# Decoder layer: quantised products with the weights' scaling on GpSimd, row norms and the first round's last outputs on ScalarE, and 16-bit halves of the rounded words turned in place

## The chip, the cores and the metric

The kernel runs on one core of a Trainium2 chip. The metric is the time of one execution on the device, in microseconds (us), as the median of several runs. The engines named below are TensorE (PE in the rows), VectorE (DVE), ScalarE (ACT), GpSimd (POOL) and SyncE (SP), which issues the DMAs. Each has its own instruction stream; semaphores order them.

## What is computed

The input x has four batches of 512 rows and 512 columns. Three blocks are added to it, each on a layer norm of what came before: an attention with low-rank projections and rotary parts, then a quantised expert per batch, then a top-2 mixture of eight experts. The change touches the second:

```
def smooth_quant_linear(x, w):
    s  = sqrt(max(amax_x_by_column, 1e-6) / max(amax_w_by_column, 1e-6)); s = max(s, 1e-6)
    xs, ws  = x / s, w * s
    x_scale = max(row max |xs|, 1e-6) / 127      # w_scale in the same way, from ws
    x_q = clip(round(xs / x_scale), -127, 127)   # w_q in the same way
    return x_q @ w_q.T * x_scale * w_scale.T

h = smooth_quant_linear(layernorm(x), fside[b])      # 512 columns in, 512 out
gate, up = split(h)
y = smooth_quant_linear(silu(gate) * up, ctx[b])     # 256 columns in, 512 out
x = x + y
```

## The kernel before, in words

Attention runs first and ends with projections of output rows, which VectorE adds to x (`add_y`). Its last projections and the beginning of the quantised stage are interleaved by hand in the functions called `tail`. After the quantised stage the mixture of experts runs over 16 row tiles of 128 rows.

The quantised stage works on two batches at a time: round r = 0, 1, linear layer l = 0, 1 (512 or 256 input columns, `LIN`), batch u = 0, 1 of the round. The list `HALVES` orders them as (r, l, u) = (0,0,0), (0,0,1), (0,1,0), (0,1,1), (1,0,0) and so on: eight halves. PSUM banks 4u to 4u+3 belong to batch u. Each engine has a loop over `HALVES`, written out in order; in it, `preceding(h)` is the half before and `succeeding` of that one is the next layer of the other batch, whose channel maxima are found meanwhile. The time at which one half's input products begin on VectorE is taken as its start below, and the halves are numbered 1 to 8.

What happens to one half:

- `channels` (TensorE, L822) turns the rows of inputs and of weights by transposes in 32-bit words; `scales` (VectorE, L663) takes the maxima by column (L675), joins them (L679), and computes the factor with a root on GpSimd (`root`, L452). `spread` (L839, matmul at L845) puts 1/s and s on all partitions, into two banks.
- `quantise` (VectorE, L695): kind 0 multiplies the input rows by 1/s in place (L709, four tiles), takes the maximum of each row (L711), and makes the scale and its reciprocal (L712, L713). Kind 1 does the same for the weights and writes the products to `HF[u]`.
- ScalarE's `rounded` (L525, L534) multiplies by the reciprocal and adds 12582912, which rounds to a whole number in a 32-bit word; `whole` (L536, L544) subtracts it and writes bf16 into a buffer (`QX[u]` for inputs, the space of the raw weights for weights).
- `quantised_t` (TensorE, L849, L857) turns these bf16 rows with `identb`, and `transposed` (ScalarE, L547, L554) copies them from PSUM to `QXT` and `QWT`. `row_scale` (L861) spreads the weights' row scales, `output_scales` (L558) copies them to `WSB`.
- `layer` (TensorE, L869, L876) multiplies. `outputs` (VectorE, L715, L721), called in the next half, scales by row and column in one operation out of PSUM into `HF[u]`.
- After layer 0, `silu` (ScalarE, L562) and `gate_product` (GpSimd, L463, L466) make the input of layer 1. After layer 1, `residual` (GpSimd, L470, L474) adds `HF[u]` to x; the last one is on VectorE (L727).
- The norm of a round's rows: `norm_stats` (L631) and `norm_batch` (L642) on VectorE, a root on GpSimd (L460), `norm_rows` (L654, L659) on VectorE, four tiles. For round 1 it stands in the middle of `scales`.

VectorE's order in a half is: input products, weight products, outputs of the half before, norm batch if the next layer is a first one, scales of the next. ScalarE's is: round inputs, copy them, round weights, silu, copy out the turned inputs, copy the weights, output scales, copy out the turned weights; at the end of halves 3 and 4 a cast of expert weights of 4096 columns (L520).

Of the kernel before, what the change touches and what calls it, by code (L numbers as in the profile page):

```python
# [17 lines left out]
B, L, D = 4, 512, 512  # L18
# [13 lines left out]
ROUND = 12582912.0  # L32
# [3 lines left out]
def decoder_layer(nc, x, fside, ctxw, w_qa, q_norm_w, w_qb, w_kva, kv_norm_w, w_kvb, w_o,  # L36
# [16 lines left out]
    with es:  # L53
# [243 lines left out]
        QX = [take(TB * D, bf16) for _ in range(2)]  # L297
# [25 lines left out]
        qeps, qrs = sm[1][:, 70:74], sm[1][:, 74:78]  # L323
# [22 lines left out]
        qx_r, qw_r, v_bc, l_mm, l_out = (sem(n) for n in ("qx_r", "qw_r", "v_bc", "l_mm", "l_out"))  # L346
# [36 lines left out]
        def rounded_rows(l, u, kind):  # L383
            return QX[u] if kind == 0 else (WF[u] if l == 0 else WC[u]).bitcast(bf16)[:, 0:TB * D]
# [65 lines left out]
        def later_pool(pool):  # L450
# [25 lines left out]
            for u in range(2):  # L476
                first_root(0, u)
            for r, l, u in HALVES:
                if l == 0:
                    gate_product(r, u)  # L480
                    root(r, 1, u)
                else:
                    if r + 1 < B // 2:
                        first_root(r + 1, u)
                    if r + 1 < B // 2 or u == 0:
                        residual(r, u)
# [28 lines left out]
        def later_act(act):  # L515
# [6 lines left out]
            def rows_of(l, u, kind):  # L522
                return (NX[u] if l == 0 else AG[u]) if kind == 0 else HF[u]

            def rounded(r, l, u, kind):  # L525
# [4 lines left out]
                rows, iv = rows_of(l, u, kind), IV[u][kind]  # L530
                act.wait_ge(own, li * 4 + 4)
# [3 lines left out]

            def whole(r, l, u, kind):  # L536

                wid, li = LIN[l][0], layer_of(r, l, u)
                made, done = ((x_q, qx_r), (w_q, qw_r))[kind]
                stride = wid if kind == 0 else D  # L540
                rows = rows_of(l, u, kind)
                for t in range(TB):
                    act.wait_ge(made, li * TB + t + 1)
                    act.activation(rounded_rows(l, u, kind)[:, t * D:t * D + wid], rows[:, t * stride:t * stride + wid],  # L544
                                   ACT.Copy, bias=-ROUND).then_inc(done, 1)

            def transposed(r, l, u, kind):  # L547
# [4 lines left out]
                for k in range(2):  # L552
                    act.wait_ge(tr, li * TB + 2 * k + 2)
                    act.activation(dst[u].rearrange("p (c t q) -> p t c q", c=DC, t=TB)[:, 2 * k:2 * k + 2, 0:c],  # L554
                                   bankb[4 * u + k].rearrange("p (t c q) -> p t c q", t=2, c=DC)[:, :, 0:c],
                                   ACT.Copy).then_inc(te, 1)
# [62 lines left out]
        def later_dve(dve, tail):  # L619
# [22 lines left out]
            def norm_batch(r, u):  # L642

                s = r * 2 + u
                dve.wait_ge(q_stat, 2 * s + 2)
                dve.memset(qcar, 0.0)
# [3 lines left out]
                dve.wait_ge(q_agg, s + 1)  # L650
                dve.tensor_scalar(qeps, qmv.rearrange("p (t a) -> p t a", a=2)[:, :, 1], 1e-5, None, ALU.add)\
                    .then_inc(q_var, 1)

            def norm_rows(r, u):  # L654

                s = r * 2 + u
                dve.wait_ge(q_rstd, s + 1)
                for t in range(TB):
                    dve.tensor_scalar(NX[u][:, t * D:(t + 1) * D], xall(batch_of(r, u) * TB + t),  # L659
                                      qmv[:, 2 * t:2 * t + 1], qrs[:, t:t + 1], ALU.subtract, ALU.mult)\  # L660
                        .then_inc(q_norm, 1)

            def scales(r, l, u, beside=None):  # L663
# [6 lines left out]
                for t in range(2 * TB):  # L670
                    if t == TB and l == 0 and r > 0:
                        norm_rows(r, u)
# [22 lines left out]
            def quantise(r, l, u, kind):  # L695
# [3 lines left out]
                vlink = chain(own_, li, 4)  # L699
                src = (NX[u] if l == 0 else AG[u]) if kind == 0 else (WF[u] if l == 0 else WC[u])  # L700
                dst, sc = ((src, XM[u]), (HF[u], WM[u]))[kind]
                m3 = src.rearrange("p (t n) -> p t n", t=TB)
                d3 = dst.rearrange("p (t n) -> p t n", t=TB)
                iv = IV[u][kind]
                dve.wait_ge(v_bc, li * 2 + 1 + kind)
                if l == 0 and kind == 1 and r > 0:
                    dve.wait_ge(x2_made, r * 2 - 1 + u)
                for t in range(TB):
# [1376 lines left out]
```

## Time and profile before

| | us |
|---|---|
| median of three runs | 1169.33 (1169.28 to 1170.31) |
| profiled execution, span from the first to the last instruction | 1169.4 |
| busy: TensorE matmuls | 980.4 (84%) |
| busy: VectorE | 959.2 (82%) |
| busy: ScalarE | 678.1 (58%) |
| busy: GpSimd | 296.4 (25%) |

The profiled execution has no separate time on record; its span stands for it. Busy is the sum of the instructions' durations on an engine. These shares are means over attention (to about 890 us), the quantised stage (to 1046.8 us) and the mixture (to the end), which have different limits.

### The profile page before, as it was taken

The numbers are of one execution on the slowest core, as the hardware profiler recorded it, in microseconds if no ns is written. First come the engines' busy times: TensorE is split into PE (matmuls) and PEld (weight loads), VectorE is DVE, ScalarE is ACT, GpSimd is POOL, SyncE is SP. The second block draws the span as 40 slices with busy tenths as digits, with TensorE's granted clock in tenths as the row PEclk, the third lists the DMA queues.
The fourth block names the chain that finished last, engine by engine and source line by source line (L and its number), as shares of the span: only waits on it lengthen the run. The fifth ranks groups of instructions, "written<-read, shape, count | busy, mean of one in ns | idle before, by whom it ended". The sixth has DMA issues, their size and how long they took to land.

```text
span 1169.4 us, 18715 instructions
## 1 busy us (share of the span) xinstructions
PE 980.4 (84%) x6106; PEld 574.0 (49%) x6124; DVE 959.2 (82%) x2669; ACT 678.1 (58%) x1449; POOL 296.4 (25%) x524
## 2 busy tenths in 40 slices
PE   0446667899999999999999999999978655559997
PEld 0234444555555555555555555555545544435553
DVE  5757749989989888989998988888868898866885
ACT  1446557667667666756666666656512676754442
POOL 1036533223223223222322222213100113221211
PEclk9769779999999999999999999999989888769999
DMA  9300003433323336334335244336363520001333
GB/s 350 139 1 1 1 8 73 75 59 71 71 59 67 66 62 142 62 64 69 65 68 138 55 68 60 64 67 140 68 218 86 168 91 19 0 1 36 84 80 91
DMA packets 217328, 90.78 MB, mean 78 GB/s; under 512 B 191496, under 2 KB 202760, under 8 KB 216720
## 3 DMA queue, kind: packets, MB, share of 16 engines
q1 hardware_dynamic: 217232, 89.58, 33.5%
q8 instruction: 50, 0.82, 0.3%
q14 instruction: 46, 0.38, 0.1%
HBM read 36.06 MB, written 7.34 MB: 37 GB/s over the span
## 4 chain that ended last, share of the span: by engine, by line
PE 53%; DVE 30%; ACT 6%; issue 5%; POOL 3%; DMA 3%; SPq 0%; DVEq 0%; ACTq 0%; POOLq 0%
PE bank L1930 13%; PE bank L1880 8%; PE bank L1915 6%; PE bank L1828 3%; PE bank L1859 3%; DVE arena L709 2%; PE bank L1898 2%; DVE arena L711 2%; PE bank L1901 2%; PE bank L1899 2%; PE bank L1900 2%; PE bank L1902 2%; DVE arena L791 2%; DVE arena L675 2%; DVE arena L1529 2%
## 5 line engine op out<-in xcount | busy, mean ns | idle before, releaser
L1218 ACT ACTIVATE arena<-bank,arena,scal 128x128 f32<-128x128 f32 (+3 forms) x256 | 157.7, 616 | 112.7 <-POOL arena L1059 111.6
L1930 PE MATMUL bank<-arena 128*128 128x512 f16 x768 | 179.1, 381 | 1.9 <-DVE arena L1562 1.9
L1536 DVE SCALAR_TENSOR_TENSOR arena<-arena 128x128 f16<-128x128 f32 (+3 forms) x256 | 142.2, 555 | 9.1
L1059 POOL TENSOR_TENSOR arena<-arena,scal 128x1 f32<-128x1 f32 x256 | 51.7, 203 | 347.4 <-DVE arena L1512 345.7
L1880 PE MATMUL bank<-arena 128*128 128x512 f16 x576 | 137.6, 385 | 0.0
L1529 DVE TENSOR_SCALAR arena<-arena 128x128 f16<-128x128 f32 (+3 forms) x256 | 125.4, 490 | 7.4 <-DVE arena L1521 0.8
L1512 DVE TENSOR_REDUCE arena<-bank 128x1 f32<-128x128 f32 (+3 forms) x256 | 123.7, 483 | 7.8 <-PE bank L1903 6.7
L1915 PE MATMUL bank<-arena 128*128 128x512 f16 (+3 forms) x768 | 117.7, 304 | 11.5 <-DMA arena<-arena 5.8
L1930 PEld LDWEIGHTS bank<-arena 128*128 128x128 f16 x768 | 72.9, 98 | 81.0 <-issue 4.4
L1915 PEld LDWEIGHTS bank<-arena 128*128 128x128 f16 x768 | 71.8, 99 | 63.0 <-issue 16.5
L1237 ACT ACTIVATE arena<-bank 32x512 f32<-32x512 f32 x128 | 75.3, 588 | 26.0 <-PE bank L1859 24.7
L1898 PE MATMUL bank<-arena 128*128 128x128 f16 (+3 forms) x256 | 77.0, 301 | 9.1 <-DVE arena L1429 5.0
L1880 PEld LDWEIGHTS bank<-arena 128*128 128x128 f16 x576 | 54.4, 99 | 55.8 <-issue 3.5
L1249 ACT ACTIVATE arena<-arena 64x512 f16<-64x512 f32 x128 | 79.9, 624 | 1.2
L1902 PE MATMUL bank<-arena 128*128 128x128 f16 (+3 forms) x256 | 76.9, 300 | 0.0
L1900 PE MATMUL bank<-arena 128*128 128x128 f16 (+3 forms) x256 | 76.9, 300 | 0.0
L1901 PE MATMUL bank<-arena 128*128 128x128 f16 (+3 forms) x256 | 76.9, 300 | 0.0
L1899 PE MATMUL bank<-arena 128*128 128x128 f16 (+3 forms) x256 | 76.9, 300 | 0.0
L1228 ACT ACTIVATE arena<-bank 128x512 f16<-128x512 f32 x64 | 38.2, 596 | 65.8 <-PE bank L1880 65.5
L835 PE MATMUL bank<-identf,arena 128*128 128x128 f32 x192 | 37.7, 355 | 40.8 <-DVE arena L721 35.9
L1828 PE MATMUL bank<-arena 128*128 128x384 f16 (+1 forms) x384 | 54.8, 303 | 18.1 <-DVE arena L1386 15.7
L1064 POOL TENSOR_TENSOR arena<-arena 128x512 f32<-128x512 f32 x32 | 44.9, 1404 | 94.2 <-ACT arena L1237 94.1
(201 smaller groups left out, 2049.5 us busy)
## 6 DMA issues: line engine op xcount, KB each, us to landing
arena<-in_L_attn_w_qb SPq DMA_DIRECT2D x1, 4608.0 KB, 21.6
arena<-arena SPq DMA_TRANSPOSE x272, 2.7
arena<-in_x SPq DMA_DIRECT2D x4, 1024.0 KB, 6.9
arena<-in_L_attn_w_o SPq DMA_DIRECT2D x1, 4096.0 KB, 31.9
arena<-in_fside_BxS2xS SPq DMA_DIRECT2D x4, 1024.0 KB, 8.8
arena<-in_L_ffn_w SPq DMA_DIRECT2D x8, 512.0 KB, 7.6
out<-arena SPq DMA_DIRECT2D x16, 256.0 KB, 2.3
arena<-in_x SPq DMA_DIRECT2D x12, 256.0 KB, 3.0
```

The source lines that it names most:

```text
L1218: act.activation(pf(k), banks[S_BANKS[G % 3]][:, 0:n], ACT.Exp, bias=NB[:, k:k + 1], scale=sc_exp, accum_out=SUM[:, k:k + 1]).then_inc(s_e ...
L1512: dve.tensor_reduce(NEGM[:, (g & 3):(g & 3) + 1], banks[S_BANKS[G % 3]][:, 0:n], AX.X, ALU.max, negate=True).then_inc(s_max, 1)
L1529: dve.tensor_scalar(ph_part(k, 0), pf(k).rearrange("p (t c) -> p t c", c=P), R4[:, k:k + 1], None, ALU.mult).then_inc(s_hi, 1)
L1536: dve.scalar_tensor_tensor(out=ph_part(k, 1), in0=pf(k).rearrange("p (t c) -> p t c", c=P), scalar=R4[:, k:k + 1], in1=ph_part(k, 0), op0= ...
L1880: last = pe.matmul(banks[Q_BANK][:, :], wq(a, c, (i & 7) * 2 + h), ct(bp, b, c, 0, L), start=(k == 0), stop=(k == 3 * QC - 1))
L1898: pe.matmul(bank[:, 0:n], qn(h, 0, q, P), ct(bp, 0, QC, 0, n), start=True, stop=False)
L1899: pe.matmul(bank[:, 0:n], qn(h, 0, q, P), ct(bp, 1, QC, 0, n), start=False, stop=False)
L1900: pe.matmul(bank[:, 0:n], qn(h, 1, q, P), ct(bp, 0, QC, 0, n), start=False, stop=False)
L1901: pe.matmul(bank[:, 0:n], qr(j, h, q, P), kr(bp, 0, 0, n), start=False, stop=False)
L1902: pe.matmul(bank[:, 0:n], qr(j, 2, q, P), kr(bp, 1 + h, 0, n), start=False, stop=False)
L1915: last = pe.matmul(banks[O_BANK][:, kt * P:L], cn(bp, a, kt), pt(h, b, kt, kt * P, L - kt * P), start=(kt == 0 and n == 0), stop=(kt == TB ...
L1930: last = pe.matmul(banks[Y_BANK][:, :], ot(gp, a, k, (q & 3) * P, P), wo(b, gp * GH + k), start=(k == 0 and n == 0), stop=(k == GH - 1 and ...
```

## The change

The weight products of `quantise` move to GpSimd (`weight_products`), which cannot read them from the PSUM bank, so ScalarE first copies the factors into a buffer `SSB` (`weight_factors`). The norm rows move to ScalarE (`norm_rows`), as x * rstd + (-mean * rstd), with the second term from GpSimd (`norm_factors`). The outputs of layer 1 of round 0 are made by ScalarE (scaled by row, `scaled_outputs`) and then GpSimd (scaled by column, `output_rows`). The constant added in rounding becomes 12582912 + 26112, so that the low 16 bits of the 32-bit word, read as fp16, are 1536 plus the whole number. TensorE turns these halves where they lie, every second 16-bit word (`rounded_tile`), with `ident16`; ScalarE subtracts 1536 in the copy out of PSUM. `whole` and its eight copies a half, and the buffer `QX`, go. VectorE's order in a half is now: input products, then the outputs of the half before or the norm batch, then the row maxima of the weights, then scales.

```diff
-ROUND = 12582912.0
+SHIFT = 1536.0
+ROUND = 12582912.0 + 26112.0
...
+        def rounded_tile(l, u, kind, t, q):
+            o = t * (LIN[l][0] if kind == 0 else D) + q * P
+            return scaled_rows(l, u, kind).bitcast(fp16).rearrange("p (n h) -> p n h", h=2)[:, o:o + P, 0]
+        def outputs_on_act(r, l):
+            return l == 1 and r + 1 < B // 2
...
             if after is not None:
-                sp.wait_ge(w_t, after * TB + TB)
+                sp.wait_ge(w_prod, after * TB + TB)
...
@@ later_pool @@
+            def norm_factors(r, u):
+                s = r * 2 + u
+                pool.wait_ge(q_var, s + 1)
                 pool.tensor_tensor(qrs, qeps, half, ALU.pow).then_inc(q_rstd, 1)
+                pool.wait_ge(q_rstd, 2 * s + 1)
+                pool.tensor_tensor(qnr, qneg, qrs, ALU.mult).then_inc(q_rstd, 1)
+            def weight_products(r, l, u):
+                wid, li = LIN[l][0], layer_of(r, l, u)
+                src = WF[u] if l == 0 else WC[u]
+                pool.wait_ge(ssb_made, li + 1)
+                if l == 1:
+                    pool.wait_ge(act_m, (r * 2 + u) * TB + TB)
+                elif r > 0:
+                    pool.wait_ge(x2_made, r * 2 - 1 + u)
+                for t in range(TB):
+                    pool.tensor_tensor(HF[u][:, t * D:t * D + wid], src[:, t * wid:(t + 1) * wid],
+                                       SSB[u][:, 0:wid], ALU.mult).then_inc(w_prod, 1)
+            def output_rows(r, u):
+                for t in range(TB):
+                    pool.wait_ge(l_out, layer_of(r, 1, u) * TB + t + 1)
+                    pool.tensor_tensor(HF[u][:, t * D:(t + 1) * D], HF[u][:, t * D:(t + 1) * D], WSB[u],
+                                       ALU.mult).then_inc(o_row, 1)
...
+            norm_factors(0, 0)
+            root(0, 0, 0)
+            norm_factors(0, 1)
+            for h in HALVES:
+                weight_products(*h)
+                prev = preceding(h)
+                after = (0, 0, 1) if prev is None else succeeding(prev)
+                if prev is not None and prev[1] == 0:
+                    gate_product(prev[0], prev[2])
+                if prev is not None and prev[1] == 1 and after is not None:
+                    norm_factors(after[0], after[2])
+                    output_rows(prev[0], prev[2])
+                if after is not None:
+                    root(*after)
+                if prev is not None and prev[1] == 1:
+                    residual(prev[0], prev[2])
...
@@ later_act @@
+            def weight_factors(r, l, u):
+                act.wait_ge(v_bc, li * 2 + 2)
+                act.activation(SSB[u][:, 0:wid], banks[4 * u + 3][:, 0:wid], ACT.Copy).then_inc(ssb_made, 1)
+            def norm_rows(r, u):
+                act.wait_ge(q_rstd, 2 * s + 2)
+                for t in range(TB):
+                    act.activation(NX[u][:, t * D:(t + 1) * D], xall(batch_of(r, u) * TB + t), ACT.Identity,
+                                   bias=qnr[:, t:t + 1], scale=qrs[:, t:t + 1]).then_inc(q_norm, 1)
+            def scaled_outputs(r, l, u):
+                for t in range(TB):
+                    act.wait_ge(l_mm, li * TB + t + 1)
+                    act.activation(HF[u][:, t * D:(t + 1) * D], out_bank(u, t)[:, :], ACT.Copy,
+                                   scale=XM[u][:, t:t + 1]).then_inc(l_out, 1)
...
+            norm_rows(0, 0)
+            norm_rows(0, 1)
             for h in HALVES:
+                weight_factors(r, l, u)
+                if prev is not None and outputs_on_act(*prev[0:2]):
+                    scaled_outputs(*prev)
                 rounded(r, l, u, 0)
-                whole(r, l, u, 0)
-                rounded(r, l, u, 1)
                 if prev is not None and prev[1] == 0:
                     silu(prev[0], prev[2])
+                rounded(r, l, u, 1)
                 transposed(r, l, u, 0)
-                whole(r, l, u, 1)
+                if prev is not None and outputs_on_act(*prev[0:2]):
+                    norm_rows(prev[0] + 1, prev[2])
                 output_scales(r, l, u)
                 transposed(r, l, u, 1)
...
@@ later_dve @@
                 if prev is not None:
                     quantise(r, l, u, 0)
+                    if not outputs_on_act(*prev[0:2]):
+                        outputs(*prev)
+                    elif after is not None:
+                        norm_batch(after[0], after[2])
                 quantise(r, l, u, 1)
-                if prev is None:
-                    scales(0, 0, 1)
-                else:
-                    outputs(*prev)
-                    after = succeeding(prev)
-                    if after is not None:
-                        if after[1] == 0:
-                            norm_batch(after[0], after[2])
-                        scales(*after, beside=(1, after[2]) if after[0:2] == (0, 1) else None)
+                if after is not None:
+                    scales(*after, beside=(1, after[2]) if after[0:2] == (0, 1) else None)
```

In `quantise`, kind 1 no longer multiplies; it waits for `w_prod` and takes the row maxima. In both layers the transposes of rounded rows (`quantised_t`) wait for `x_q` and `w_q`, the rounding itself.

## Rows read from the trace of the kernel before

**Rows 1.** Windows, halves 2 to 7: start:end and length, busy by engine, PEclk.

```profile
910.92:932.37 21.45, 13.00 (x87) 9.65 (x88) 19.24 (x38) 15.13 (x26) 3.48 (x5) 0.76 0.44 121
932.37:948.69 16.32, 11.10 (x64) 8.15 (x66) 14.96 (x39) 11.05 (x26) 3.48 (x5) 0.79 0.17 60
948.69:968.07 19.38, 10.38 (x74) 8.46 (x73) 16.60 (x44) 13.65 (x23) 3.68 (x4) 0.91 0.52 163
968.07:991.85 23.78, 12.16 (x97) 10.21 (x97) 20.99 (x44) 14.26 (x22) 6.69 (x5) 0.86 0.00 1
991.85:1012.75 20.90, 12.90 (x85) 9.87 (x85) 17.07 (x33) 14.27 (x25) 6.46 (x6) 0.76 0.00 0
1012.75:1028.51 15.76, 11.62 (x65) 8.62 (x65) 12.78 (x33) 10.32 (x26) 3.48 (x5) 0.78 0.00 1
```

**Rows 2.** Chain that ended last, halves 1 and 2: start us, us, what.

```profile
889.62 1.78 PE bank L845 x16
...
897.37 2.40 DVE arena L709 x4
...
910.92 2.49 DVE arena L709 x4
...
916.14 2.38 DVE arena L709 x4
...
921.18 2.74 DVE arena L721 x4
```

**Rows 3.** The same chain, half 2's tail to half 7's start.

```profile
928.89 0.25 DVE arena L679 x2
...
932.37 1.32 DVE arena L709 x4
...
935.35 1.31 DVE arena L709 x4
...
943.90 0.42 DVE arena L675
...
957.80 2.38 DVE arena L675 x4
960.19 1.82 DVE arena L659 x4
...
964.44 0.28 DVE arena L679 x2
...
968.07 2.49 DVE arena L709 x4
...
1009.92 0.25 DVE arena L679 x2
```

**Rows 4.** Timeline of ScalarE: start us, us, engine, line, operation, shapes, count.

```profile
947.36 3.63 ACT L520 ACTIVATE arena<-arena 128x4096 bf16<-128x4096 f32 x1
951.71 1.70 ACT L534 ACTIVATE arena<-arena 128x256 f32<-128x256 f32 x4 [0.72 <-DVE arena L713]
973.32 2.56 ACT L534 ACTIVATE arena<-arena 128x512 f32<-128x512 f32 x4 [4.59 <-DVE arena L713]
983.45 1.94 ACT L554 ACTIVATE arena<-bank 128x1024 bf16<-128x1024 bf16 x2 [2.44 <-PE bank L857]
1049.62 0.81 ACT L591 ACTIVATE arena<-arena 128x512 f32<-128x512 f32 x1 [6.17 <-POOL arena L498]
```

**Rows 5.** L1064 on GpSimd, in attention: count, ns min/median/max.

```profile
L1064 POOL TENSOR_TENSOR arena<-arena x32: 1263/1270/1662, 153.4 to 830.7; 128x512 f32<-128x512 f32 x32
```

**Rows 6.** Timeline of GpSimd, gate products and a residual.

```profile
940.45 2.78 POOL L466 TENSOR_TENSOR arena<-arena 128x256 f32<-128x256 f32 x4 [9.94 <-ACT arena L565]
...
966.52 4.54 POOL L474 TENSOR_TENSOR arena<-arena 128x2048 f32<-128x2048 f32 x1
```

**Rows 7.** Lines by form, 890 to 1047 us, transposes: busy us, mean ns.

```profile
L835 PE MATMUL bank<-identf,arena 128*128 128x128 f32 x160 | 33.4, 371 | 40.6 <-DVE arena L721 35.9 <-DVE arena L675 2.1 <-DVE arena L659 1.7
...
L857 PE MATMUL bank<-identb,arena 128*128 128x128 bf16 x192 | 18.6, 251 | 4.5 <-ACT arena L544 3.9
```

More of the change, by code:

```diff
@@ L296, in decoder_layer @@
         place[0] = odd_at
-        QX = [take(TB * D, bf16) for _ in range(2)]
+        SSB = [take(D) for _ in range(2)]
         QXT = [take(DC * L, bf16) for _ in range(2)]
@@ L322, in decoder_layer @@
         pcar = sm[0][:, 84:85]
-        qeps, qrs = sm[1][:, 70:74], sm[1][:, 74:78]
+        qeps, qrs, qneg, qnr = (sm[1][:, 70 + 4 * k:74 + 4 * k] for k in range(4))
         place[0] = moe
@@ L345, in decoder_layer @@
         x_q, x_t, x_te, w_q, w_t, w_te = (sem(n) for n in ("x_q", "x_t", "x_te", "w_q", "w_t", "w_te"))
-        qx_r, qw_r, v_bc, l_mm, l_out = (sem(n) for n in ("qx_r", "qw_r", "v_bc", "l_mm", "l_out"))
+        ssb_made, w_prod, o_row, v_bc, l_mm, l_out = (
+            sem(n) for n in ("ssb_made", "w_prod", "o_row", "v_bc", "l_mm", "l_out"))
         w_row, x_own, w_own = (sem(n) for n in ("w_row", "x_own", "w_own"))
@@ L529, in rounded @@
                 stride = wid if kind == 0 else D
-                rows, iv = rows_of(l, u, kind), IV[u][kind]
-                act.wait_ge(own, li * 4 + 4)
+                rows, iv = scaled_rows(l, u, kind), IV[u][kind]
+                act.wait_ge(own, li * 4 + 4 if kind == 0 else li * 3 + 3)
                 for t in range(TB):
@@ L534, in rounded @@
                     act.activation(w, w, ACT.Copy, bias=ROUND, scale=iv[:, t:t + 1]).then_inc(made, 1)
[L536 to L545, printed above, removed]
             def transposed(r, l, u, kind):
@@ L645, in norm_batch @@
                 dve.wait_ge(q_stat, 2 * s + 2)
+                if s > 0:
+                    dve.wait_ge(q_norm, s * TB)
                 dve.memset(qcar, 0.0)
@@ L650, in norm_batch @@
                 dve.wait_ge(q_agg, s + 1)
+                dve.tensor_scalar(qneg, qmv.rearrange("p (t a) -> p t a", a=2)[:, :, 0], -1.0, None, ALU.mult)
                 dve.tensor_scalar(qeps, qmv.rearrange("p (t a) -> p t a", a=2)[:, :, 1], 1e-5, None, ALU.add)\
                     .then_inc(q_var, 1)
[L654 to L661, printed above, removed]
             def scales(r, l, u, beside=None):
@@ L698, in quantise @@
                 own_ = (x_own, w_own)[kind]
[L699 to L708, printed above, removed]
-                    last = dve.tensor_tensor(d3[:, t, 0:wid], m3[:, t, :], banks[4 * u + 2 + kind][:, 0:wid], ALU.mult)
-                vlink(last)
+                vlink = chain(own_, li, 4 - kind)
+                sc, iv = (XM[u], WM[u])[kind], IV[u][kind]
+                d3 = scaled_rows(l, u, kind).rearrange("p (t n) -> p t n", t=TB)
+                if kind == 0:
+                    dve.wait_ge(v_bc, li * 2 + 1)
+                    if l == 0 and r > 0:
+                        dve.wait_ge(l_out, layer_of(r - 1, 1, u) * TB + TB)
+                    for t in range(TB):
+                        last = dve.tensor_tensor(d3[:, t, 0:wid], d3[:, t, 0:wid], banks[4 * u + 2][:, 0:wid], ALU.mult)
+                    vlink(last)
+                else:
+                    dve.wait_ge(w_prod, li * TB + TB)
                 vlink(dve.tensor_reduce(sc, d3[:, :, 0:wid], AX.X, ALU.max, apply_absolute_value=True))
@@ L727, in outputs @@
                     dve.tensor_tensor(X, X, HF[u], ALU.add).then_inc(x2_made, 1)
-            tail(norm_stats, norm_batch, norm_rows, scales, quantise)
+            tail(norm_stats, norm_batch, scales, quantise)
             for h in HALVES:
@@ L850, in quantised_t @@
                 wid, li = LIN[l][0], layer_of(r, l, u)
-                made, done = ((qx_r, x_t), (qw_r, w_t))[kind]
+                made, done = ((x_q, x_t), (w_q, w_t))[kind]
                 for t in range(TB):
@@ L1755, in _, with tail @@
             out_lo(2 * NPAIR - 1)
-            def tail(norm_stats, norm_batch, norm_rows, scales, quantise):
+            def tail(norm_stats, norm_batch, scales, quantise):
                 add_y(NPAIR - 5)
@@ L1761, in tail @@
                 norm_batch(0, 0)
-                norm_rows(0, 0)
                 add_y(NPAIR - 4)
```

40 lines of the change are left out of this document (13 added, 27 removed).

## Prediction

> **What bounds the kernel now.** Of the span the change touches only the quantised stage, from about 890 us to 1046.8 us. I read it first by stages of one half each [rows 1]. The stage has eight halves; half 1 overlaps the end of attention, halves 2 to 7 take 21.45, 16.32, 19.38, 23.78, 20.90 and 15.76 us, half 8 the rest. In each VectorE is the fullest engine (19.24 of 21.45, 12.78 of 15.76), ScalarE follows (15.13, 10.32), GpSimd is nearly empty (3.5 to 6.7). Busy shares alone don't say what ends a half, so the chain of waits comes next [rows 2, 3]. It runs on VectorE almost without a break: the products and reductions of the input rows, the same for the weight rows, the outputs of the half before (2.74), the channel reductions (0.43 for 256 columns, 2.38 for four of 512), then the short tail of small operations, a root on GpSimd and a spread on TensorE, after which the next half begins. That tail is 3.48 us long in halves 2 and 3 (928.89 to 932.37, norm statistics lie in it), 2.83 in halves 6 and 7 (1009.92 to 1012.75), 3.63 ahead of a half of 512 columns (964.44 to 968.07) [rows 3]. So what leaves VectorE counts fully, until a chain through ScalarE and GpSimd becomes longer.
>
> **What the change removes from VectorE.** The weight products: 2.38 us in each half of 512 columns, 1.31 in each of 256 [rows 2, 3]. The outputs of the first round's second products in halves 4 and 5: 2.74 each [rows 2]. The norm rows in halves 4 and 5: 1.82 each [rows 3]; two more such groups lie under TensorE's last projections and free nothing. Added are one 4-wide negation per norm batch, some 0.1. Sum for halves 1 to 7: 4 x 2.38 (1, 2, 5, 6) + 3 x 1.31 (3, 4, 7) + 2 x 4.56 = 22.6 us.
>
> **What it adds elsewhere.** ScalarE copies the factors out of PSUM, and makes the outputs and norm rows: four tiles of 512 go in 2.56 us as the scaling by a column does now, four of 256 in 1.70; a copy out of the transposes of 512 columns takes 1.94 [rows 4]. It loses eight whole-number copies a half. GpSimd makes four products of a row tile. The same operation takes 1.27 us at the median of 32, once 1.66 [rows 5]; four of 256 go in 2.78 and the residual of 2048 columns in 4.54 [rows 6], so one of 512 goes in 1.24 and four in 4.95 by the line through these two. I take 4.95, nearest to the median; the upper end is 6.6 (4 x 1.66).
>
> I now lay out each half, from the start of its input products (time 0) to that of the next. Input part: 5.22 us (910.92 to 916.14) or 2.98 (932.37 to 935.35). Weight part without the products: 921.18 - 916.14 - 2.38 = 2.66, or, like the input part, 2.98 - 1.32, about 1.6 [rows 2, 3].
>
> *Half 1.* The factors are spread at 891.4 (889.62 + 1.78), copied by 892.0, products done by 897.0; VectorE gets there at 897.37, after the last projection [rows 2]. Nothing is late: it saves 2.4.
>
> *Half 2.* Factors copied by 1.5, products done at 6.5. VectorE: 5.22, outputs to 7.96, weight part to 10.6 (the products are 1.4 early), eight reductions of 0.43 to 14.0, tail 3.48. The gate products wait on GpSimd behind the weight products and behind silu, and are done at about 10; the transposes that need them are 0.5 later, before VectorE asks. 17.5, against 21.45: 3.95 saved, of which 1.7 is VectorE's present wait for those transposes.
>
> *Half 3.* 2.98 + 2.74 + 1.6 + 3.43 + 3.48 = 14.2, against 16.32: 2.1. The outputs come before the weight part now, so they could wait for the layer of half 2; its last tile lands at about 4.3, when the last output begins.
>
> *Half 4.* First place with a new wait. ScalarE ends half 3 with a cast of 3.63 us [rows 4]: scales of the weights known at 7.3, then 1.70 of rounding, 1.0 for the turned inputs, 0.6 for the output scales, 1.4 for the turned weights with TensorE ahead of them, and the cast, 15.6 in all, which is 1.4 of half 4. The factors' copy stands behind the cast, then four products of 256 columns: done at 4.55. VectorE is ready at 3.6 (2.98, and some 0.6 for a norm batch of seven operations like the two small ones of 0.28) [rows 3] and waits 1.0. Weight part to 6.2. Then ScalarE rounds the weights (to 8.0), copies the turned inputs (to 9.0) and only then makes the norm rows (to 11.5). Behind them wait the transposes (0.45) and the last reduction (0.6): 12.6, where VectorE alone would be at 6.2 + 4.8 = 11.0. With the tail of 3.63: 16.3, against 19.38: 3.1 saved. If norm rows run at the 0.81 of the lone operation with a column as bias [rows 4], it is 0.7 less.
>
> *Half 5.* GpSimd's queue is norm factors, output rows, root, residual, and the weight products stand behind the residual, which begins at the root's end (12.6 + 1.95 for small operations and root) and takes 4.7: over at 19.3, which is 3.0 of half 5. Products done at 8.05, where VectorE is ready at 5.9: it waits 2.2. Weight part to 10.7, rounding to 13.3, turned copies to 15.2, norm rows to 17.7, transposes and last reduction to 18.8, tail to 22.5, against 23.78: 1.3 saved.
>
> *Half 6.* Again behind a residual (over at 3.0): products at 8.0; VectorE with the outputs is there at 7.96. 7.96 + 2.7 + 3.43 + 2.83 = 16.95, against 20.90: 3.9.
>
> *Half 7.* 2.98 + 2.74 + 1.6 + 3.43 + 2.83 = 13.6, against 15.76: 2.2.
>
> *Half 8.* The outputs (2.74) now stand ahead of the weight part on the path to the last rounding; the product (1.31) and one set of whole-number copies (at most the 1.70 that four of 256 take) leave it. Even: 0.
>
> Sum: 2.4 + 3.95 + 2.1 + 3.1 + 1.3 + 3.9 + 2.2 = 18.95 us. So 22.6 leave VectorE, some 4.5 of present idle time goes too (VectorE's waits for transposes, which the gate products no longer hold up), and 8.1 come back: waits in halves 4 (1.0 and 1.6) and 5 (2.2 and 3.3 from the weight part to the last norm row). The profiled span is 1169.4 and the median of the runs 1169.33, so they can be taken as one. 1169.4 - 18.95 = 1150.4; for hand-overs between engines that I counted at nothing I add 0.6: **1151**.
>
> **Unknown costs.** The turned halves: TensorE reads every second 16-bit word. No row shows that. Nearest are the 16-bit transposes at 251 ns and those of 4-byte words at 371 [rows 7]. At the second price 16 transposes gain 0.12 x 16 = 1.9 in modelled duration, about 0.9 in pace; most lie beside VectorE, and where they don't (halves 3 and 8, with 4 and 5 possibly) it costs 0 to 2 us in all. I take 0, the price of the row with the same word and shape. A gain is excluded: nothing is read or turned less. GpSimd's products at 1.66 would add 1.7 to each of halves 1, 5 and 6, 0.3 to half 2 and 0.8 to half 4: 6.2. Norm rows at 0.81 for each: 1.4 in halves 4 and 5 together.
>
> The residual of 4.54 us on GpSimd starts at 966.52 [rows 6], and VectorE's products at 968.07, which run inside it, take 2.49, as against 2.38 at 916.14 and 1.31 for half as many columns [rows 2, 3]: no lock is to be seen, only 0.1. The Trainium skill ("SBUF — State Buffer", on the two sides and their ports) says that VectorE in a two-port mode, or with two SBUF inputs, and GpSimd exclude each other for a whole instruction. VectorE's long operations here read at most one operand from SBUF, so by that rule they are free, and the sum stays; its small ones could wait, which is rival C. On strided reads the same page says that 16-byte lines give full speed with two hits or more in a line; every second halfword has four, so the sum stays at the price of contiguous reads. No row here shows either case.
>
> **Rivals.** *A*, the forecast: VectorE's load sets the halves but for 4 and 5. 1149 to 1153.5. *B*: the chain through GpSimd and ScalarE is longer than laid out (products at up to 1.66, norm rows at 0.81, transposes at the wide price): 6.2 + 1.4 + 2 = 9.6 at most, half of it likely, 1153.5 to 1159. For it: half 5 and 6 already end on GpSimd. Against: the 32 samples lie at 1.27 beside a busy VectorE. *C*: VectorE's tiny operations wait for a running GpSimd instruction. Scales of the inputs fall into the weight products in all halves; each can wait up to 1.24 us, 0.6 on average, twice a half: 7 x 2 x 0.6 = 8, less the part that halves 4 and 5 idle anyway, so 1157. The page above is what would make this so; the trace shows the residual ending no operation late. *D*, the other side: weight products on GpSimd become the bound, because beside ScalarE and VectorE they run at half speed. Each 0.1 us on a tile costs 0.4 in halves 1, 5, 6, in half 2 beyond its 1.4 of slack, and half as much in those of 256 columns beyond theirs. The saving is used up at about 2.3 us a tile; at 2.5 the time is 1174. Only the absence of a sample of 512 columns in this stage speaks for it. *E*: my waits in halves 4 and 5 are too pessimistic (ScalarE runs ahead): 1147 to 1149. *F*: nothing is gained, since the halves are held by something other than VectorE; the chain, which stands on it for most of each half, speaks against.
>
> **How the numbers follow.** A 0.66, B 0.16, C 0.05, E 0.07, D 0.04, F 0.02. A measurement tells 0.2% (2.3 us) from nothing. A, B, C and E are faster: 0.94; F is same: 0.02; D slower: 0.04. The range holds A and the near parts of B and E: 1148 to 1156.5.
>
> **What would show it.** Right: halves of about 17.5, 14.2, 16.3, 22.5, 17.0 and 13.6 us; VectorE waiting for GpSimd at the weight reduction of halves 4 (1.0) and 5 (2.2) alone; channel reductions waiting for norm rows in 4 and 5; GpSimd tiles spaced by 1.24. Wrong: such waits in halves 2, 3 or 7, tiles over 1.5, small VectorE operations far over 0.2, or transposes of the rounded rows slower than now by half.

## The result, and the profile after

| | us |
|---|---|
| before, median | 1169.3 |
| changed, median of four runs | 1159.78 (1158.07 to 1160.7) |
| ratio | 0.991 (0.9894 to 0.9925) |
| changed, profiled execution: its own time, and its span | 1159.43, 1157.6 |

The change is 9.5 us faster, where 18.3 were forecast, and the time lies above the range. In the changed kernel's runs the time is 1.8 us more than the span. So the profiled execution before, with a span of 1169.4, took about 1171.2, which is 1.9 above its median, and a sum made against its span is not one made against the median. Outside the quantised stage (attention and the mixture) the traces of all kernels here differ by up to 6 us with no pattern, so I compare the stage itself: from the first spread of half 1 (L845 before, L883 after) to the end of the last sum (L727, L767). It went from 157.25 to 144.46 us, 12.8 less; the forecast was 18.95. A second trace of the changed kernel (e5 below) gave 146.79.

Windows of the changed kernel, halves 2 to 8: start:end and length, busy time (and number of instructions) of PE, its weight loads, DVE, ACT and POOL, then the granted clock and two DMA columns, as in [rows 1]:

```profile
906.73:923.32 16.59, 12.73 (x88) 8.50 (x87) 16.25 (x33) 10.41 (x18) 8.47 (x9) 0.90 0.87 256
923.32:937.20 13.88, 9.32 (x67) 6.06 (x66) 13.53 (x35) 9.93 (x20) 6.27 (x9) 1.00 0.00 1
937.20:956.37 19.17, 13.53 (x75) 10.52 (x74) 12.99 (x33) 14.11 (x24) 11.51 (x13) 0.73 0.50 165
956.37:980.43 24.06, 14.15 (x98) 11.48 (x97) 15.70 (x32) 17.52 (x23) 16.68 (x14) 0.79 0.00 0
980.43:997.30 16.87, 12.02 (x86) 8.42 (x85) 14.69 (x29) 10.04 (x18) 11.42 (x10) 0.90 0.00 1
997.30:1010.46 13.16, 10.40 (x66) 7.57 (x65) 11.20 (x29) 8.58 (x20) 6.27 (x9) 0.87 0.01 2
1010.46:1032.21 21.75, 10.02 (x44) 4.89 (x42) 15.95 (x19) 9.73 (x16) 7.42 (x6) 0.69 0.00 0
```

Forecast were 17.5, 14.2, 16.3, 22.5, 16.95, 13.6, and half 8 as before (18.2). Halves 2, 3, 6 and 7 came out, a little better. Half 4 is 2.9 us over, half 5 1.6, half 8 3.5. In halves 4 and 5 VectorE is busy for 13.0 of 19.2 and 15.7 of 24.1: it is no longer the fullest in half 5, and it waits in both (below). In half 8 it seems busy for 15.95, and that is a false reading, as the next rows show. They are VectorE's timeline of the changed kernel in halves 4, 6 and 8, the small operations on the row scales:

```profile
943.43 1.20 DVE L753 TENSOR_SCALAR arena<-arena 128x4 f32<-128x4 f32 x1
...
985.27 0.80 DVE L753 TENSOR_SCALAR arena<-arena 128x4 f32<-128x4 f32 x1
...
1017.49 3.59 DVE L753 TENSOR_SCALAR arena<-arena 128x4 f32<-128x4 f32 x1
1021.11 0.18 DVE L754 RECIPROCAL arena<-arena 128x4 f32<-128x4 f32 x1
```

and GpSimd's at the second and third of these moments:

```profile
983.56 4.95 POOL L485 TENSOR_TENSOR arena<-arena 128x512 f32<-128x512 f32 x4
...
1016.55 4.50 POOL L507 TENSOR_TENSOR arena<-arena 128x2048 f32<-128x2048 f32 x1
```

An operation on four columns takes 3.59 us and ends at 1021.08, just after the residual does (1021.05). The one at 985.27 ends at 986.07; the second of the four products ends at 983.56 + 2 x 1.24 = 986.04. It counts as busy while it waits. All sixteen of this line (count, ns min/median/max), first in the trace before, then in the changed kernel, where twelve of the sixteen take more than 0.2 us:

```profile
L712 DVE TENSOR_SCALAR arena<-arena x16: 169/170/171, 895.6 to 1034.2; 128x4 f32<-128x4 f32 x16
```

```profile
L753 DVE TENSOR_SCALAR arena<-arena x16: 169/391/3586, 893.7 to 1017.5; 128x4 f32<-128x4 f32 x16
```

The order of work in half 4 (from 937.20) and half 5 (from 956.37) is read on ScalarE: roundings (L569) and norm rows (L592):

```profile
944.88 1.70 ACT L569 ACTIVATE arena<-arena 128x256 f32<-128x256 f32 x4 [1.70 <-DVE arena L754]
946.49 1.05 ACT L578 ACTIVATE arena<-bank 128x512 bf16<-128x512 f16 x2
947.44 2.92 ACT L592 ACTIVATE arena<-arena 128x512 f32<-128x512 f32 x4
...
967.23 2.56 ACT L569 ACTIVATE arena<-arena 128x512 f32<-128x512 f32 x4 [2.40 <-DVE arena L754]
969.69 1.91 ACT L578 ACTIVATE arena<-bank 128x1024 bf16<-128x1024 f16 x2
971.50 2.92 ACT L592 ACTIVATE arena<-arena 128x512 f32<-128x512 f32 x4
```

and behind them TensorE's transposes, with its idle time before them in brackets:

```profile
948.30 3.67 PE L873 MATMUL bank<-identf,arena 128*128 128x128 f32 x16 [4.79 <-ACT arena L592]
...
972.36 3.68 PE L873 MATMUL bank<-identf,arena 128*128 128x128 f32 x16 [7.07 <-ACT arena L592]
```

The same 16 transposes took 2.03 us in the kernel before. The granted clock is the first number of the last three in these windows of the changed kernel, 0.50 of full speed, which is the lower of its two levels, 1.2 GHz; before, behind the norm rows, it was 1.00:

```profile
948.30:952.00 3.70, 3.70 (x18) 3.70 (x19) 2.08 (x3) 2.06 (x3) 0.00 (x0) 0.50 0.49 163
972.30:976.00 3.70, 3.64 (x17) 3.65 (x18) 2.07 (x3) 2.12 (x4) 0.00 (x0) 0.50 0.00 0
```

VectorE waits 2.24 us in half 4 and 3.95 in half 5 for the first of them, and the last reduction ends at 15.5 and 20.4 us of the half, where 12.6 and 18.8 were forecast.

### The profile page after: what moved, and what is told of

Its sections match the earlier page's. It is cut to its first block, busy times and chain, and to the rows that moved or that the text cites. A ratio compares the mean times of both kernels' runs of the same rounds, so it can differ in the third digit from the quotient of the medians.

```text
span 1157.6 us, 18702 instructions
## 1 busy us (share of the span) xinstructions
PE 981.6 (85%) x6124; PEld 570.6 (49%) x6124; DVE 938.2 (81%) x2617; ACT 670.5 (58%) x1417; POOL 337.7 (29%) x568
## 4 chain that ended last, share of the span: by engine, by line
PE 59%; DVE 20%; ACT 7%; issue 5%; POOL 5%; DMA 3%; SPq 0%; DVEq 0%; ACTq 0%; POOLq 0%
PE bank L1966 13%; PE bank L1916 8%; PE bank L1951 6%; PE bank L971 5%; PE bank L1864 3%; PE bank L1895 3%; PE bank L980 2%; PE bank L1934 2%; PE bank L1935 2%; PE bank L1936 2%; PE bank L1938 2%; PE bank L1937 2%; DVE arena L1567 2%; DVE arena L1574 2%; DVE scal L1711 1%
## 5 line engine op out<-in xcount | busy, mean ns | idle before, releaser
L1966 PE MATMUL bank<-arena 128*128 128x512 f16 x768 | 179.2, 381 | 1.9 <-DVE arena L1600 1.9
L1916 PE MATMUL bank<-arena 128*128 128x512 f16 x576 | 137.4, 384 | 0.0
L1895 PE MATMUL bank<-arena 128*128 128x512 f16 x288 | 67.4, 379 | 0.0
## 6 DMA issues: line engine op xcount, KB each, us to landing
arena<-in_L_attn_w_qb SPq DMA_DIRECT2D x1, 4608.0 KB, 21.3
```

The costliest lines, as they stand in the source:

```text
L1895: last = pe.matmul(banks[R_BANK][:, :], wr(b, c, i & 7), ct(bp, a, c, 0, L), start=(k == 0), stop=(k == 3 * QC - 1))
L1916: last = pe.matmul(banks[Q_BANK][:, :], wq(a, c, (i & 7) * 2 + h), ct(bp, b, c, 0, L), start=(k == 0), stop=(k == 3 * QC - 1))
L1966: last = pe.matmul(banks[Y_BANK][:, :], ot(gp, a, k, (q & 3) * P, P), wo(b, gp * GH + k), start=(k == 0 and n == 0), stop=(k == GH - 1 and ...
```

## The experiments

The expectations name three theories. Theory 1, exclusion: small VectorE operations wait for a running GpSimd instruction. Theory 2, clock: TensorE is slow behind its idle time. Theory 3, order: the norm rows stand too late in ScalarE's order. The diffs are cut to the lines that matter.

Halves and stage of each profiled run, in us; half 1 is counted from the first spread.

| | 1 | 2 | 3 | 4 | 5 | 6 | 7 | 8 | stage | median |
|---|---|---|---|---|---|---|---|---|---|---|
| before | 21.5 | 21.4 | 16.3 | 19.5 | 23.8 | 20.9 | 15.8 | 18.2 | 157.25 | 1169.3 to 1170.9 |
| changed | 19.0 | 16.6 | 13.9 | 19.2 | 24.1 | 16.9 | 13.2 | 21.8 | 144.46 | 1159.8 |
| e1 | 19.0 | 16.5 | 13.3 | 18.1 | 24.1 | 16.5 | 12.7 | 18.2 | 138.40 | 1152.0 |
| e2 | 19.4 | 17.7 | 14.0 | 20.0 | 23.8 | 16.9 | 13.0 | 18.3 | 143.23 | 1155.7 |
| e3 | 19.1 | 18.0 | 13.9 | 19.7 | 22.9 | 16.9 | 13.0 | 21.6 | 145.00 | 1158.0 |
| e4 | 19.8 | 17.7 | 14.1 | 16.9 | 19.4 | 16.9 | 13.0 | 21.7 | 139.44 | 1150.7 |
| e5 | 19.1 | 18.0 | 13.9 | 20.1 | 23.9 | 17.0 | 13.0 | 21.8 | 146.79 | 1157.1 |
| e6 | 21.5 | 19.0 | 15.0 | 19.1 | 24.1 | 19.5 | 14.2 | 21.6 | 153.94 | 1165.8 |
| e7 | 19.8 | 17.7 | 14.1 | 20.3 | 22.6 | 16.9 | 13.0 | 21.7 | 146.05 | 1159.9 |
| e8 | 19.0 | 16.7 | 13.3 | 15.0 | 19.4 | 16.7 | 12.7 | 18.2 | 131.03 | 1143.7 |
| e9 | 21.5 | 21.3 | 16.3 | 19.4 | 23.7 | 20.9 | 15.7 | 17.0 | 155.80 | 1168.6 |
| e10 | 19.0 | 17.1 | 13.8 | 19.3 | 24.7 | 16.9 | 13.0 | 21.7 | 145.52 | 1159.7 |
| e11 | 19.2 | 18.0 | 13.9 | 20.1 | 24.2 | 17.3 | 13.1 | 18.5 | 144.26 | 1158.5 |
| e12 | 19.3 | 16.5 | 13.3 | 15.9 | 18.4 | 16.5 | 12.7 | 16.3 | 128.98 | 1141.7 |

The times of e1, e2, e4, e5 and e6 lie 0.2 to 1.3 us below the ranges that were expected for them; e7 and e11 miss theirs by more, upwards.

**e1, the row maxima through PSUM.**

```diff
-vlink(dve.tensor_reduce(sc, d3[:, :, 0:wid], ...))
-vlink(dve.tensor_scalar(sc, sc, 1e-6, 1.0 / QMAX, ALU.max, ALU.mult))
+raw = banks[4 * u + 2 + kind][:, 0:TB]
+vlink(dve.tensor_reduce(raw, d3[:, :, 0:wid], ...))
+vlink(dve.tensor_scalar(sc, raw, 1e-6, 1.0 / QMAX, ALU.max, ALU.mult))
```

> The changed kernel, but the row maxima (L752) are written to a free PSUM bank, and the small operation L753 (times 1/127) reads them there. Theory 1, exclusion: L753, which reads and writes SBUF, waits until the GpSimd instruction that runs has ended (0.80 us in half 6, 1.20 in half 4, 3.59 in half 8, where the residual of 4.54 runs). With its input in PSUM it takes about 0.2 each time, half 8 is 3.4 us shorter, the stage about 6 us shorter, 1153 to 1155. Rival: the long L753 is a wait for a semaphore or for its own input, the reduction: then it is as long as now and the time stays at 1159 to 1160.

1151.97 us, ratio 0.9848 (0.9831 to 0.9864). The same operation, now with its input in a bank, in e1:

```profile
L754 DVE TENSOR_SCALAR arena<-bank x16: 161/162/163, 893.9 to 1015.1; 128x4 f32<-128x4 f32 x16
```

All sixteen take 0.16 us beside the same GpSimd work. In half 8 it starts at 1015.09, inside the residual (1014.14 to 1018.65), and is over at 1015.25. So L753 waited neither for a semaphore nor for the reduction, but because its input and its output both lay in SBUF while GpSimd ran. Half 8 is 3.6 us shorter, the stage 6.1 (8.4 against e5). Theory 1 is shown. One small operation of the norm batch, still from SBUF to SBUF, goes on waiting in e1 (L703, 1.26 us in half 5).

**e2, a later residual in half 8.**

```diff
+if r + 1 == B // 2:
+    pool.wait_ge(w_own, layer_of(1, 1, 1) * 3 + 3)
```

> The changed kernel, but the residual of half 8 (GpSimd, 4.54 us) waits until the weights' scales of half 8 are known, so that it no longer runs beside L753. Theory 1: L753 of half 8 falls from 3.59 to about 0.2 or, if it meets a weight product, to under 0.9; half 8 goes from 21.8 to about 18.4 and the whole is 3 to 3.5 us faster, 1156 to 1157. Rival: half 8 is long because the outputs now stand ahead of the weights' scales: no change, 1159 to 1160.

1155.67 us, ratio 0.9869 (0.9853 to 0.9886), and half 8 18.3 us. L753 there:

```profile
1019.32 0.17 DVE L755 TENSOR_SCALAR arena<-arena 128x4 f32<-128x4 f32 x1
```

So half 8 is even with before (18.2), as the forecast had it, and the residual was what cost time. Even is a balance: by e12 the new order of outputs and weights' scales costs 1.9 us by itself, and what left the half makes up for it.

**e3, TensorE kept busy.**

```diff
+if after is not None and after[0:2] == (1, 0):
+    for k in range((34, 50)[after[2]]):
+        pe.transpose(banks[4 * h[2] + 2][:, k % 4 * P:(k % 4 + 1) * P], identf, identf)
```

> The changed kernel, with 34 (half 4) and 50 (half 5) transposes of the identity into a free bank on TensorE ahead of the transposes of the norm rows, where TensorE now stands idle for 4.8 and 7.1 us. Their output is not used. Theory 2, clock: the 16 transposes L873 behind the idle time take 3.67 us in place of 2.03 because the granted clock has fallen (0.72 and 0.62 in these stretches); kept busy, they follow the norm rows at 0.73 us, the last reduction ends 1.2 us earlier in each half, in all 1.5 to 2.5 us, 1157 to 1158. Rival: they are paced by the norm rows alone (0.73 us each) and nothing is gained, or the added work delays them: 1159 to 1162.

1158.03 us, ratio 0.9895 (0.9878 to 0.9911). In e3 the transposes behind the added ones are no longer slow:

```profile
952.70 2.77 PE L873 MATMUL bank<-identf,arena 128*128 128x128 f32 x16
...
975.88 2.77 PE L873 MATMUL bank<-identf,arena 128*128 128x128 f32 x16 [1.61 <-ACT arena L592]
```

2.77 us in place of 3.67, the pace of the norm rows, and the clock in these stretches of e3 is the full 2.4 GHz:

```profile
952.70:955.40 2.70, 2.56 (x18) 1.84 (x18) 1.98 (x3) 2.06 (x3) 0.01 (x1) 1.00 0.64 208
975.88:978.60 2.72, 2.57 (x18) 1.86 (x19) 2.00 (x3) 2.06 (x3) 0.00 (x0) 1.00 0.00 0
```

Half 5 is 1.2 us shorter than in the changed kernel (1.0 than in e5), half 4 0.4 shorter than in e5 but not than in the first trace. The times show no gain: 1158.03, against 1159.78 and 1157.06 for the changed kernel. That the slower clock stretches the transposes is shown; what it costs is about 1 us in half 5 and not resolved in half 4.

**e4, norm rows first.** On ScalarE `norm_rows` goes ahead of `rounded(r, l, u, 1)`.

```diff
+if prev is not None and outputs_on_act(*prev[0:2]):
+    norm_rows(prev[0] + 1, prev[2])
 rounded(r, l, u, 1)
 transposed(r, l, u, 0)
-if prev is not None and outputs_on_act(*prev[0:2]):
-    norm_rows(prev[0] + 1, prev[2])
```

> The changed kernel, with norm rows on ScalarE ahead of the rounding of the weights in halves 4 and 5. Theory 3, order: halves 4 and 5 end late (19.1 and 24.1 us where 16.3 and 22.5 were forecast) because the norm rows stand behind the weights' scales, their rounding and a copy. Put first they end about 3 us earlier in half 4 and 5 us in half 5, VectorE goes on almost without a wait, and the whole is 6 to 8 us faster, 1152 to 1154. Rival: the weights' rounding, now later, holds the turned weights and the layer, and these take the place: under 3 us gained, 1157 to 1160.

1150.68 us, ratio 0.9841 (0.982 to 0.9861). Half 4 falls to 16.9 and half 5 to 19.4. In half 5 of e4, first ScalarE:

```profile
965.23 2.93 ACT L592 ACTIVATE arena<-arena 128x512 f32<-128x512 f32 x4 [0.90 <-POOL arena L473]
968.06 2.55 ACT L569 ACTIVATE arena<-arena 128x512 f32<-128x512 f32 x4
```

then VectorE, whose eight reductions now run without a break:

```profile
966.59 4.92 DVE L716 TENSOR_REDUCE arena<-bank 128x4 f32<-128x512 f32 x8
```

Theory 3 is shown: what holds these halves back is the place of the rows in ScalarE's order, 2.3 us in half 4 and 4.7 in half 5 (3.2 and 4.6 against e5).

**e5, the changed kernel again.**

> The changed kernel without an edit, beside the next three on the same chip, for comparison with them. 1158 to 1161, the quantised stage (first spread to last sum) 144 to 146 us.

1157.06 us (1154.91 to 1162.57), ratio 0.989 (0.987 to 0.991), and a stage of 146.79, where 144 to 146 was expected. The trace, of the slowest of its runs, has a stage 2.3 us longer than the first. The difference is in half 2 and half 4. Half 2, L753 in the changed kernel's first trace and in e5:

```profile
911.56 0.17 DVE L753 TENSOR_SCALAR arena<-arena 128x4 f32<-128x4 f32 x1
```

```profile
914.54 1.30 DVE L753 TENSOR_SCALAR arena<-arena 128x4 f32<-128x4 f32 x1
```

Both begin some 0.05 us before a product ends (911.61 in the first trace, 914.59 in e5). In the first trace L753 goes ahead of the next product, in e5 it waits for the whole of it. So the kernel's time depends on a phase, from 0 to 1.1 us at such a place; in e1, e8 and e12, which have no such wait, half 2 is 16.5 to 16.7.

**e6, weight products on VectorE again.** Without `weight_factors` and `weight_products`:

```diff
-    dve.wait_ge(w_prod, li * TB + TB)
+    for t in range(TB):
+        dve.tensor_tensor(d3[:, t, 0:wid], src[:, t, :], banks[4 * u + 3][:, 0:wid], ALU.mult).then_inc(w_prod, 1)
+    dve.wait_ge(w_prod, li * TB + TB)
```

> The changed kernel, but the weight products are made by VectorE out of the PSUM bank as before, and the factors' copy on ScalarE and the products on GpSimd are gone. On VectorE this adds 4 x 2.4 + 4 x 1.3 = 14.8 us. Theory 1: beside that the waits of L753 for weight products go (about 3 us on the path) and those for the products themselves (1.0 and 1.2 in halves 4 and 5, and the 3 us by which half 5's products wait for a residual), so only 7 to 10 of the 14.8 show: 1166 to 1169. The residual of half 8 meets L753 1.3 us later, at 2.3 in place of 3.6. Rival: the waits cost little, and nearly all 14.8 show: 1172 or more, slower than before the change.

1165.77 us, ratio 0.9971 (0.9961 to 0.9981), near what theory 1 had: of the 14.8 us that moved to GpSimd, 6 to 8.7 show, where 7 to 10 were expected. L753 (here L758) is 0.17 in thirteen of sixteen. It is 1.25 and 0.34 beside GpSimd's output rows (from 949.98 and 973.34), and 2.15 beside the residual of half 8, met 1.3 us later:

```profile
1028.90 2.15 DVE L758 TENSOR_SCALAR arena<-arena 128x4 f32<-128x4 f32 x1
```

**e7, norm rows of round 1 on VectorE.** In `scales`, at t == TB, as before; no `norm_rows` in ScalarE's loop.

```diff
+if t == TB and l == 0 and r > 0:
+    norm_rows(r, u)
```

> The changed kernel, but the norm rows of round 1 (halves 4 and 5) are made by VectorE in the middle of the channel reductions, as before. It adds 2 x 1.82 to VectorE. Theory 3: on ScalarE these rows stand behind the weights' rounding and a copy, and end the half; on VectorE they start as soon as the reductions of the weights are done, about 2 us earlier in half 4 and 3 to 4 in half 5, so undoing this part of the change makes it faster: 1153 to 1157. Rival: VectorE is still what ends these halves, and it is 2 to 3.6 us slower: 1161 to 1164.

1159.87 us, ratio 0.9928 (0.9909 to 0.9948): neither theory's time, a miss. The rows in half 4 of e7, and GpSimd's output rows:

```profile
949.17 2.79 DVE L709 TENSOR_SCALAR arena<-arena 128x512 f32<-128x512 f32 x4
```

```profile
945.38 4.93 POOL L491 TENSOR_TENSOR arena<-arena 128x512 f32<-128x512 f32 x4
```

They start at 10.7 us of the half, and take 2.79 in place of 1.82 [rows 3]: the first of them, begun at 949.17, lasts 1.43 us, 0.28 beyond the end of GpSimd's output row (950.31). The same exclusion holds for them, and they have one operand in SBUF and their output there. A gain in half 5 (1.4 to 1.5) is offset by half 4's, which is no better.

**e8, the edits of e1 and e4 together.**

> The edits of e1 and e4 together: L753 reads from PSUM, norm rows ahead of the weights' rounding. Each alone gave 1152.0 and 1150.7 against 1159.8. Theories 1 and 3 name different stretches (halves 3, 6, 8 and part of 4 against the end of halves 4 and 5), so the gains add but for 1 us in half 4: 1143 to 1145. Rival: they are one and the same wait, seen twice: 1149 to 1151.

1143.69 us, ratio 0.9786 (0.9769 to 0.9802): 16.1 us under the changed kernel, where e1 and e4 alone gave 7.8 and 9.1. The gains add but for 0.8, so the two causes are separate.

**e9, the halves alone.** The kernel before, without `whole`, with `rounded_tile`, `ident16` and the constant of the change.

```diff
-whole(r, l, u, 0)
-whole(r, l, u, 1)
...
-    rounded_rows(l, u, kind)[:, ...], identb[:, :])
+    rounded_tile(l, u, kind, t, q), ident16[:, :])
```

> The kernel before, with one part of the change alone: the whole-number copies go, TensorE turns the low 16-bit halves of the rounded words where they lie, ScalarE subtracts 1536 in the copy out of PSUM. If a read of every second halfword costs nothing (16 transposes L857 in 1.06 us at 2.4 GHz, 1.9 at 1.2), only the copy in the last chain of half 8 (1.2 us) and a little beside it go: 1 to 2.5 us faster, 1167 to 1169. Rival: the strided read has the price of 4-byte words (mean 371 ns against 251): 0 to 1 us slower.

1168.64 us, ratio 0.9981 (0.9966 to 0.9995). Half 8 is 1.2 us shorter, all others within 0.1 of before. The transposes, in the changed kernel:

```profile
L895 PE MATMUL bank<-ident,arena x192: 216/219/314, 897.5 to 1024.4; 128*128 128x128 f16 x192
```

219 ns at the median, the same as L857 before and the same line in e9: reading every second halfword costs nothing here.

**e10, outputs of halves 4 and 5 on VectorE.** `outputs_on_act` false, no `output_rows`; norm batch after the outputs.

```diff
-    return l == 1 and r + 1 < B // 2
+    return False
```

> The changed kernel, but the outputs used in halves 4 and 5 are made by VectorE as before, and GpSimd's output rows are gone. By the forecast's sum they were worth 2 x 2.74 = 5.5 us. Theory 3: they were not, since VectorE waits in both halves for products and norm rows; the weights' scales come 0.5 to 1.5 us later and the halves with them: 0 to 3 us slower than the changed kernel, 1157 to 1161. Rival: all 5.5 show, 1163 to 1165.

1159.66 us, ratio 0.9907 (0.9883 to 0.9932), against 0.991 and 0.989: this part of the change, 5.5 us in the forecast's count of what leaves VectorE, is worth about 2 at most by these ratios in the changed kernel. VectorE waits in these halves anyway (2.24 and 3.95 us, above), which is the likely reason.

**e11, residuals in four instructions.**

```diff
-pool.tensor_tensor(X, X, HF[u], ALU.add).then_inc(x2_made, 1)
+for t in range(TB):
+    last = pool.tensor_tensor(X[:, t * D:(t + 1) * D], X[:, t * D:(t + 1) * D], HF[u][:, t * D:(t + 1) * D], ALU.add)
+last.then_inc(x2_made, 1)
```

> The changed kernel, with each residual on GpSimd in four instructions of 512 columns in place of one of 2048. Theory 1: the wait of L753 ends with the GpSimd instruction that runs, so in half 8 it is at most 1.2 us in place of 3.6, and half 8 is 2.4 to 3.4 us shorter: 1154 to 1157. Rival: VectorE waits for GpSimd's queue or for the whole residual: L753 stays at 3.6, or longer, 1158 to 1161.

1158.52 us, ratio 0.9889 (0.9864 to 0.9914): the time is a miss. The gain of 3.3 us in half 8 does not show in a median of four runs that spread as widely as those of the same kernel do (e5: 1154.91 to 1162.57). Half 8 itself came out as expected: 18.5 us, and L753 of that half, here L756:

```profile
1021.20 0.35 DVE L756 TENSOR_SCALAR arena<-arena 128x4 f32<-128x4 f32 x1
```

while the four run from 1020.26 on, and the first ends at about 1021.5. The wait ends with the instruction that runs (1021.20 + 0.35 = 1021.55), not with GpSimd's queue.

**e12, e8 with the last half in the old order.** In half 8 VectorE takes the weights' row maxima ahead of the outputs of half 7.

```diff
     quantise(r, l, u, 0)
+    if h == HALVES[-1]:
+        quantise(r, l, u, 1)
     ...
-quantise(r, l, u, 1)
+if h != HALVES[-1]:
+    quantise(r, l, u, 1)
```

> e8 with VectorE's order in half 8 as before the change: row maxima of the weights ahead of the outputs of half 7. The products are done 0.7 us after the inputs' scales, so the weights' scales are known 1.9 us earlier, and half 8, in which they start the last chain, is 1.5 to 2 us shorter: 1141.5 to 1142.5. Rival: the outputs, later, hold the residual or the last chain: no gain, 1143.5 or more.

1141.68 us (1140.43 to 1143.81), ratio 0.9749 (0.9728 to 0.977); half 8 16.3 in place of 18.2. This is the fastest version, some 28 to 29 us under the kernel before. In the windows of its halves 4, 5 and 8 VectorE is busy for 11.0, 14.5 and 12.5 us only, so more could perhaps be had there; no run tried it:

```profile
939.22:955.16 15.94, 12.19 (x74) 8.59 (x74) 10.96 (x33) 15.69 (x24) 12.44 (x13) 0.82 0.59 198
955.16:973.53 18.37, 13.58 (x97) 11.08 (x98) 14.45 (x33) 15.66 (x23) 15.80 (x14) 0.88 0.00 0
1002.80:1019.07 16.27, 10.07 (x43) 4.89 (x42) 12.46 (x19) 9.72 (x15) 7.44 (x6) 0.64 0.00 0
```

## Why the prediction was wrong

- **What bounds the stage, and what leaves VectorE.** Right for halves 1, 2, 3, 6 and 7: 2.5, 4.8, 2.4, 4.0 and 2.6 us saved, forecast 2.4, 3.95, 2.1, 3.9 and 2.2. GpSimd's four products take 4.95, as interpolated.
- **The step that failed: the cost of VectorE's small operations beside GpSimd was put at nothing.** In the changed kernel such an operation waits to the end of the GpSimd instruction that runs: 3.4 us in half 8, 1.0 in half 4, up to 0.65 elsewhere (1.1 in e5). This is rival C's mechanism; its chance of 0.05 was too low, and its price missed the largest case, the residual of 4.5 us beside half 8. e1, e2 and e11 show it.
- **The trace before already showed it, outside the stage.** "No lock is to be seen" was read from a residual beside products that read a PSUM bank, and not even the 0.1 us is its doing: the products at 910.92 take the same 2.49 [rows 2] with GpSimd idle. These rows of the trace before are from attention: one operation of line L1529 with no long GpSimd instruction beside it, one beside an instruction of 1.27 us, and a cast of 64 columns beside one of 1.21:

```profile
200.36 0.29 DVE L1529 TENSOR_SCALAR arena<-arena 128x128 f16<-128x128 f32 x1
...
222.19 1.27 POOL L1070 TENSOR_TENSOR arena<-arena 128x512 f32<-128x512 f32 x1
222.74 0.80 DVE L1529 TENSOR_SCALAR arena<-arena 128x128 f16<-128x128 f32 x1
...
124.57 1.21 POOL L1111 TENSOR_TENSOR arena<-arena 128x512 f16<-128x512 f32 x1
124.68 1.15 DVE L1485 CAST arena<-arena 128x64 f16<-128x64 f32 x1
```

  Of the 64 of this shape 16 take 0.80 to 1.27 us in place of 0.28, and each ends 0.08 us after a GpSimd instruction; the cast takes 0.19 at the median. GpSimd waits too: of the 32 products of [rows 5], for which the prediction has "once 1.66", eleven take 1.65 to 1.66, all begun while VectorE ran L1536, which reads two operands from SBUF. From these rows rival C could have had its price and a higher chance.
- The Trainium skill ("SBUF — State Buffer", on the two sides and their ports) states that a VectorE operation in a two-port mode, or with two inputs from SBUF, and a GpSimd operation exclude each other for a whole instruction, and "Advanced Engine Details and Errata" (VectorE Performance Modes) says that the two-port mode needs source and destination in SBUF. The trace agrees with both: 3.59 us with the source in SBUF, 0.16 in PSUM. The prediction counted operands ("at most one operand from SBUF, so by that rule they are free"), although the rule has the two-port mode beside the two operands: the norm rows of e7 have one and wait. RECIPROCAL and TENSOR_REDUCE out of SBUF did not wait: 0.18 us at 894.19 in half 1, while products ran from 890.40 to 895.35, and 1.22 and 2.29 for the row maxima (L752) beside products, their durations before. No experiment here tested what sets them apart.
- **Half 4's and 5's chains were mis-sized.** The order was forecast rightly, norm rows behind rounding and copy. Half 4 ends 2.9 us late: the rows start 1.2 later than forecast (10.2 for 9.0 us of the half; 1.0 of it is L753's wait), they go at 0.73 us each, where 0.62 was taken and 0.81 given as a bound (0.4), and the transposes behind 4.8 us of idle time go at 0.85 us a tile in place of 0.45 (1.3; granted clock 0.50). In half 5, 1.6 late, the rows start when forecast (15.1 for 15.2); their pace and the slow transposes behind 7.1 us of idle time are the whole of it, and with TensorE kept busy (e3, clock 1.00) 1.2 of it goes. The forecast did not ask what TensorE does while it waits.
- **How far this accounts for the miss.** With L753's waits gone (e1) the stage is 138.40 us and the time 1151.97; the forecast was 157.25 - 18.95 = 138.30, and 1151. That agreement is partly luck: halves 4 and 5 of e1 are still 1.8 and 1.6 us over, and halves 2, 3, 6 and 7 together 3.2 under, for a reason that no run shows.
- **Unknown costs.** Strided transposes: nothing, as taken (e9). GpSimd's pace: as taken.
- **The base.** The span was equated with the median; the profiled execution lay 1.9 us above it.
- **Half 8, "even".** Right but for the lock (e2: 18.3 against 18.2).
- Still open: why the part outside the stage differs by up to 6 us between traces. With it the medians' 9.5 and the stage's 12.8 are consistent, but not derived from each other.

## What to carry to other kernels

When work moves to GpSimd, list every VectorE operation of the kinds that waited here, however small: TENSOR_SCALAR and CAST with input and output in SBUF. Each may wait for a whole GpSimd instruction, so keep these short, or read from PSUM, as e1 does. And look through the whole trace before for one operation with two durations (L1529, 0.28 and 0.80 to 1.27 us), not only through the stage that is to change. When work moves to an engine with an order of its own, its place there decides: first of what is ready, not where the code was. A busy share can hide a wait (3.59 us for four columns).

## What was not expected of the hardware

- A TENSOR_SCALAR of 128x4 from SBUF to SBUF: 0.17 us alone, up to 3.59 beside GpSimd; 0.16 in all sixteen of e1, with its source in PSUM.
- Four norm rows as TENSOR_SCALAR of 128x512: 1.82 us alone [rows 3], 2.79 when begun beside GpSimd's output rows (e7).
- ScalarE with a column for both scale and bias: four tiles of 512 in 2.92 us, with a scale alone in 2.56.
